# Attention as a stream of units with key features in place, and a second graph layer's bases added in halves beside the first layer

## What is computed

```python
xn = _layernorm(x, axis=-1)
x = x + gnn(xn) + mix(xn)          # graph layers; attention and perceptron, twice
x = x + ffn(_layernorm(x))         # memory layer: 64 rows of two tables per token

# gnn: two layers, relu between them
w = jnp.einsum('rb,bio->rio', att, basis)       # 2 relations from 30 bases of 512x512
gate = jax.nn.sigmoid(x_j @ gate_w[r, :, 0])    # for each relation
agg = jax.ops.segment_sum(msg, row)             # msg = gate * x_j @ w[r]
return agg + x @ root + bias

# mix, for each of 2 blocks, 8 heads of 64, 256 features
qp = ratio * (jnp.exp(q_dash - diag - rowmax) + 1e-4)
kp = ratio * (jnp.exp(k_dash - diag - globalmax) + 1e-4)
ctx = jnp.einsum('bhnm,bhnd->bhmd', kp, v)
o = jnp.einsum('bhmd,bhnm,bhn->bhnd', ctx, qp, 1 / (qp @ kp.sum(2)))
x = x + o @ Wo + bo; x = x + gelu(layernorm(x) @ W1 + b1) @ W2 + b2
```

## Time and profile before

| what | us |
|---|---|
| median of 3 runs (3040.13 to 3047.05) | 3040.56 |
| the profiled execution | 3042.31 |
| its span, first to last instruction | 3040.5 |
| TensorE busy | 2645.5 |
| VectorE busy | 1529.6 |
| GpSimd busy | 1021.6 |
| memory layer, from 1862 us to the end | 1178 |

### The profile page before, as it was taken

The page is one execution under the profiler, slowest core; times in us unless marked ns, Lnnn a source line. Parts: engine busy times, 40 slices in busy tenths (PEclk is TensorE's granted clock), DMA queues, the critical chain, the costliest instruction groups (busy, mean ns, idle before and its releaser), DMA issues.

```text
span 3040.5 us, 27921 instructions
## 1 busy us (share of the span) xinstructions
PE 2645.5 (87%) x8756; PEld 1455.5 (48%) x8756; DVE 1529.6 (50%) x3729; ACT 701.9 (23%) x1525; POOL 1021.6 (34%) x833
## 2 busy tenths in 40 slices
PE   3998887999199999999898887898998999998877
PEld 2664555666044444444565545554454444443322
DVE  4556457999400000000225543357666676676664
ACT  1223222211021001100235222133233333322222
POOL 0006686666000000000000000055656665665665
PEclk9998998999699999999999998999999999999999
DMA  8911416777902230243000400088988988998898
GB/s 284 276 41 4 111 1 169 207 206 216 213 29 56 66 83 0 64 116 93 7 0 0 155 0 7 7 280 314 327 308 308 337 317 302 339 328 320 320 346 331
DMA packets 243106, 523.84 MB, mean 172 GB/s; under 512 B 98857, under 2 KB 99232, under 8 KB 238850
## 3 DMA queue, kind: packets, MB, share of 16 engines
q0 software_dynamic: 161392, 348.53, 34.6%
q1 hardware_dynamic: 79072, 169.12, 17.8%
q10 hardware_dynamic: 2550, 5.12, 0.5%
HBM read 489.51 MB, written 45.34 MB: 176 GB/s over the span
## 4 chain that ended last, share of the span: by engine, by line
PE 66%; DVE 14%; issue 7%; DMA 6%; ACT 3%; POOL 1%; SPq 1%; another core or an unknown queue 1%; DVEq 0%; ACTq 0%; POOLq 0%
PE bank L1256 13%; PE bank L1029 10%; PE bank L1014 5%; DVE qv L863 4%; PE bank L1236 4%; PE bank L1246 4%; PE bank L781 3%; PE bank L561 2%; PE bank L1193 2%; PE bank L1019 2%; PE bank L573 2%; PE bank L568 2%; PE bank L592 2%; PE bank L808 2%; PE bank L1205 2%
## 5 line engine op out<-in xcount | busy, mean ns | idle before, releaser
L1156 POOL MEMSET wreg<- 64x2048 f32 x2 | 3.6, 1802 | 1106.9 <-DVE h L711 1106.9
L1256 PE MATMUL bank<-qv,stage 125*125 125x512 f32 x640 | 340.2, 623 | 37.9 <-issue 15.7
L1337 ACT ACTIVATE stage<-ident,qv 125x125 f32<-125x125 f32 x640 | 246.4, 399 | 507.9 <-DVE qv L1490 175.1
L1490 DVE SCALAR_TENSOR_TENSOR qv<-qv 125x512 f32<-125x512 f32 x320 | 237.9, 750 | 152.6 <-DMA qv<-in_L_ffn_rows,qv 69.1
L863 DVE SCALAR_TENSOR_TENSOR qv<-wreg,att_b,qv 128x2048 f32<-128x2048 f32 x120 | 276.8, 2348 | 48.8 <-DMA wreg<-in_L_gnn_basis 42.3
L287 POOL DMA_INDIRECT adj<-e_cnt,e_idx x80 | 176.3, 2204 | 310.0 <-issue 273.6
L1162 POOL DMA_INDIRECT qv<-in_L_ffn_rows,qv x160 | 162.3, 1015 | 221.3 <-DVE qv L1432 113.0
L287 POOL DMA_INDIRECT adj_b<-e_cnt,e_idx x80 | 180.7, 2258 | 71.0 <-DMA adj<-e_cnt,e_idx 39.8
L1256 PEld LDWEIGHTS bank<-qv,stage 125*125 125x125 f32 x640 | 113.6, 193 | 184.0 <-issue 121.1
L1162 POOL DMA_INDIRECT qv<-in_L_ffn_rows,biasb x160 | 163.4, 1021 | 100.8 <-PE bank L1256 74.1
L1256 PE MATMUL bank<-big,stage 125*125 125x512 f32 x320 | 167.0, 617 | 13.3 <-issue 6.4
(11 more groups left out here) (222 smaller groups left out, 4167.6 us busy)
## 6 DMA issues: line engine op xcount, KB each, us to landing
wreg<-in_L_gnn_basis SPq DMA_DIRECT2D x60, 1024.0 KB
big<-in_L_mix_W SPq DMA_DIRECT2D x4, 4096.0 KB
adj<-adj_b POOLq DMA_DIRECT2D x9, 1328.1 KB, 40.9
adj<-wreg SPq DMA_DIRECT2D x5, 2187.5 KB
adj_b<-wreg SPq DMA_DIRECT2D x5, 2187.5 KB
...
```

Source lines behind the costliest of these rows:

```text
L1256: nc.tensor.matmul(psum[7][0:P, :], diags[:, s % DRING, :], ring[s % RING][0:P, DIM:ROW], start=(s == 0), stop=(s == SLOTS - 1), skip_grou ...
L1337: nc.scalar.activation(diags[:, s % DRING, :], ident[0:P, 0:P], ACT.Relu, scale=inner[:, s:s + 1]).then_inc(p_diag, 1)
L1490: nc.vector.scalar_tensor_tensor(ring[s % RING][0:P, 0:DIM], ring[s % RING][0:P, 0:DIM], probs_of[t % 2].rearrange("p h k -> p (h k)")[:, ...
```

## The change

- `attn1`: no loop registers. The heads' squares are 8 matmuls of 250 columns with a selector as weights, ScalarE copies their result, and four transposes bring it back. The next pair's scaled transposes come after the third copy of key features and not after the fifth.
- `attn2`: the key features stay in `kdash`. The shift is the bias of eight exponentials of 256 columns a tile, in place; VectorE adds 1e-4 in two halves; TensorE reads values and features where they are. The contexts' copies are shared by VectorE and ScalarE and begin as each bank ends.
- `attn3`: 40 units in one stream, for all ten tiles. The transposes of three units of four go to bank 2, those of the fourth and the output product to bank 3. The end work of a tile stands between units of the next.
- `mlp`: only the 30 bases of layer 0 are added there, from a ring of three.
- `gcn`: the 30 bases of layer 1 are loaded as 60 halves by GpSimd, behind scatters and sums on its queue, into a ring of four, and added by VectorE in layer 0: three halves before the root add of each tile in the first half, four before each tile's aggregate add in the second. The transposes of tile t+1 stand between the relations of tile t. Layer 1 reads its input where it is. The weights and the first two tiles of x may come before the perceptron's end; layer 1's slabs may come before its first half ends; the second attention block no longer waits at its start for the stored result.

```diff
+        WREL_B = 5100
+        wrel = qv[:, :].rearrange("p (l k) -> p l k", l=2)[:, :, 0:4096].rearrange("p l (r k) -> p l r k", r=2)
...
+        HRING = 4
+        s_hload = [sem(f"half_basis_ring_{n}") for n in range(HRING)]
+        half_ring = [stage[:, 2024 + 1024 * n:3048 + 1024 * n] for n in range(HRING - 1)] + [ctx_flat[:, 0:1024]]
...
-        BLOCKS = 2 * BASES // PAIRS
-        BRING = 4
+        BLOCKS = BASES // PAIRS
+        BRING = 3
...
-                    if c == 0:
-                        pe.wait_ge(m["kd"], l * ADDS["kd"] + i * 8 + 4)
+                    if i and c < 2:
+                        pe.wait_ge(m["kd"], kd0 + 5 + c)
...
+                    else:
+                        pe.wait_ge(m["kd"], l * ADDS["kd"] + i * 8 + n + 1)
                     if n == 2:
-                        pe.wait_ge(m["k"], l * ADDS["k"] + i * KC + KC + 2)
-                    if n == 4 and not last:
+                        pe.wait_ge(m["dgc"], l * ADDS["dgc"] + i + 1)
+                        for jj in range(2):
+                            for s in range(2):
+                                mm = nc.tensor.transpose(psum[1][0:P, 256 * jj + 128 * s:256 * jj + 128 * s + 128],
+                                                         dgs[:, PT * s + P * jj:PT * s + P * jj + P], ident[:, :])
+                        mm.then_inc(m["dg_pe"], 1)
+                    if n == 4 and i < PAIRS - 1:
                         turn(i + 1)
-                    if n >= 4:
-                        pe.wait_ge(m["kd"], l * ADDS["kd"] + i * 8 + n + 1)
...
+                act.wait_ge(m["dg_mm"], l * ADDS["dg_mm"] + i + 1)
+                nc.scalar.activation(dgs, psum[0][:, 0:2 * PT], ACT.Copy).then_inc(m["dgc"], 1)
...
-                    if n == 5 and not last:
+                    if n == 3 and i < PAIRS - 1:
                         scale(i + 1)
...
         def attn2_act(act, l):
...
-            with act.Fori(0, PAIRS) as i:
-                for j in range(2):
-                    act.wait_ge(m["ctx_pe"], l * ADDS["ctx_pe"] + i * 2 + j + 1)
-                    nc.scalar.activation(v_st[:, j, :], v_aug[:, ds(i * 2 + j, 1), :, :].rearrange("p o h d -> p (o h d)"), ACT.Copy)
-                    act.wait_ge(m["ksub"], l * ADDS["ksub"] + i * 2 + j + 1)
-                    nc.scalar.activation(kfeat[:, j, :], sq1(kdash[:, ds(i * 2 + j, 1), :]), ACT.Exp).then_inc(m["kx"], 1)
+            for t in range(TILES):
+                for hh in range(HEADS):
+                    kt = kdash[:, t, FEATS * hh:FEATS * hh + FEATS]
+                    op = nc.scalar.activation(kt, kt, ACT.Exp, bias=kshift[:, t, hh:hh + 1])
+                    if hh % 4 == 3:
+                        op.then_inc(m["kx"], 1)
+            for b in (1, 3):
+                act.wait_ge(m["ctx_pe"], l * ADDS["ctx_pe"] + b + 1)
...
         def attn2_dve(dve, l):
-            def pair(i, last):
-                for j in range(2):
-                    dve.wait_ge(m["kx"], l * ADDS["kx"] + i * 2 + j + 1)
-                    nc.vector.tensor_scalar(kfeat[:, j, :], kfeat[:, j, :], EPS_K, None, ALU.add).then_inc(m["kf"], 1)
-                    if not last:
-                        subtract_k(dve, l, i * 2 + (2 + j))
-
-            with dve.Fori(0, PAIRS - 1) as i:
-                pair(i, False)
-            pair(PAIRS - 1, True)
-            dve.wait_ge(m["ctx_pe"], l * ADDS["ctx_pe"] + 2 + TILES)
-            for b in range(4):
+            for t in range(TILES):
+                for b in range(2):
...
-                    for hh in range(HEADS):
-                        mm = nc.tensor.matmul(psum[hh // 2][0:HD + 1, FEATS * (hh % 2):FEATS * (hh % 2) + FEATS],
-                                              v_st[:, j, (HD + 1) * hh:(HD + 1) * hh + HD + 1], kfeat[:, j, FEATS * hh:FEATS * hh + FEATS],
-                                              start=False, stop=True, skip_group_check=True)
...
-        QD_BANKS = (0, 1, 6, 7)
+            for t in range(TILES):
+                for hh in range(HEADS):
+                    if hh % 4 == 0:
+                        pe.wait_ge(m["kf"], l * ADDS["kf"] + 2 * t + hh // 4 + 1)
+                    mm = nc.tensor.matmul(psum[hh // 2][0:HD + 1, FEATS * (hh % 2):FEATS * (hh % 2) + FEATS],
+                                          v_aug[:, t, hh, :], kdash[:, t, FEATS * hh:FEATS * hh + FEATS],
...
+        def turn_bank(u):
+
+            return 3 if u % KC == 1 else 2
...
+                if 2 <= n < UNITS + 2:
+                    u = n - 2
+                    dve.wait_ge(m["qT_pe"], l * ADDS["qT_pe"] + u + 5)
+                    nc.vector.tensor_scalar(qfeat_t[:, u % 2, :], psum[turn_bank(u)][:, 0:4 * P], EPS_K, None, ALU.add).then_inc(m["qT"], 1)
+                if n >= 4 and n % 2 == 0 and (n - 4) // 4 < TILES:
+                    normalize((n - 4) // 4, (n - 4) % 4 // 2)
+                if n >= 10 and n % 4 == 2:
...
+                    residual((n - 10) // 4)

...
             if l == 0:
                 act.sem_inc(m["qT_pe"], 4)
...
+            def out_turn(T):
+                pe.wait_ge(m["o"], l * ADDS["o"] + 2 * T + 4)
...
+            for n in range(UNITS + 6):
+                if n < UNITS:
...
+                        pe.wait_ge(m["ctx"], l * ADDS["ctx"] + 4)
+                    pe.wait_ge(m["qx"], l * ADDS["qx"] + u + 5)
+                    if u % KC == 1 and u >= 9:
+                        pe.wait_ge(m["hat"], l * ADDS["hat"] + 2 * ((u - 9) // 4) + 3)
+                    elif u:
+                        pe.wait_ge(m["qT"], l * ADDS["qT"] + u + (1 if u % KC in (1, 2) else 2))
+                    for q in range(4):
+                        mm = nc.tensor.transpose(psum[turn_bank(u)][:, P * q:P * q + P], qfeat[:, u % 4, 128 * q:128 * q + 128], ident[0:P, 0:P])
+                    mm.then_inc(m["qT_pe"], 1)
...
+                if n >= 8 and n % 4 == 0:
+                    out_turn((n - 8) // 4)
+                if n >= 9 and n % 4 == 1:
+                    out_mm((n - 9) // 4)
...
-                    gl, b = n // (BLOCKS // 2), n % (BLOCKS // 2)
...
-                        nc.vector.scalar_tensor_tensor(wrel[:, gl, r, :], wreg[:, n % BRING, :], att_b[:, gl, ds(i * (BLOCKS // 2) + (r * BASES + b), 1)],
-                                                       wrel[:, gl, r, :], ALU.mult, ALU.add).then_inc(s_comb, 1)
+                        nc.vector.scalar_tensor_tensor(wrel[:, 0, r, :], wreg[:, n % BRING, :], att_b[:, 0, ds(i * BLOCKS + (r * BASES + n), 1)],
+                                                       wrel[:, 0, r, :], ALU.mult, ALU.add).then_inc(s_comb, 1)
...
             else:
-                sp.wait_ge(g_sem[0]["r"], 2 + TILES)
+                sp.wait_ge(g_sem[0]["r"], TILES)
             sp.dma_start(root_sb, a[f"L0_gnn_root{gl + 1}"].rearrange("(k p) n -> p k n", p=128)).then_inc(g["w"], 16)
...
-            sp.dma_start(b_g, a[f"L0_gnn_bias{gl + 1}"].partition_broadcast(P)).then_inc(g["w"], 16)
             if gl == 0:
-                with sp.Fori(0, PAIRS) as i:
-                    sp.wait_ge(g["xT_pe"], i * 2 + 2)
-                    sp.dma_start(gx, tok(xn_d)[:, ds(i * 2, 2), :]).then_inc(g["x"], 16)
-
-            def load_slab(i, j):
-                flat = slabs[gl][:, j, :, :].rearrange("p c r -> p (c r)")
+                sp.wait_ge(s_xnw, 32)
+                sp.wait_ge(m["y2_pe"], KC + KC * PAIRS)
+                for t in range(2):
+                    sp.dma_start(gx[:, t, :], tok(xn_d)[:, t, :]).then_inc(s_gx[t], 16)
+                sp.wait_ge(m["hf"], 2 + 2 * TILES)
+            sp.dma_start(b_g, a[f"L0_gnn_bias{gl + 1}"].partition_broadcast(P)).then_inc(g["b"], 16)
...
+            if gl == 1:
+                sp.wait_ge(g["r"], TILES)
+                sp.wait_ge(g_sem[0]["agg"], TILES)
+                attn_loads_sp(sp, 1)
...
+        def gcn_turn_pe(pe, gl, t):
+            g = g_sem[gl]
+            if gl == 0:
+                pe.wait_ge(s_gx[t % 2], 16 * (t // 2) + 16)
             else:
-                load_slab(0, 0)
-                sp.wait_ge(g["r"], 2 + TILES)
-                sp.wait_ge(g_sem[0]["agg"], 2 + TILES)
-                load_slab(0, 1)
...
+            for k in range(KC):
+                rows = gx[:, t % 2, 128 * k:128 * k + 128] if gl == 0 else x1[:, t, 128 * k:128 * k + 128]
+                mm = nc.tensor.transpose(psum[t % 2][:, P * k:P * k + P], rows, ident[0:P, 0:P])
+            mm.then_inc(g["xT_pe"], 1)
...
+                if gl == 0 and t == 1:
+                    pe.wait_ge(m["hf"], 2 + 2 * TILES)
+                for r in range(RELS):
+                    if t >= 2:
+                        pe.wait_ge(g["z"], 2 * (t - 2) + r + 1)
...
+                    if r == 0 and t < TILES - 1:
+                        gcn_turn_pe(pe, gl, t + 1)
+                if t >= 2:
+                    pe.wait_ge(g["r"], t - 1)
+                elif gl == 1:
+                    pe.wait_ge(g_sem[0]["out"], 2 * (TILES - 2 + t) + 1)
```

(46 more changed lines are left out.)

530 lines of the change are left out of this document (240 added, 290 removed).

## The result

The changed kernel takes **2807.88 us** (median of 4 runs, 2807.37 to 2809.99) against 3043.48 for the kernel before, a ratio of 0.9227 with a 95% interval of 0.9211 to 0.9243. The profiled execution's span is 2805.3 us; 3040.5 was that of before.

A forecast was written before the change was run, and what follows sets the result against it. TensorE, busy 87% of the span, was taken as the bound, so only its idle or slow time could be won: 53 + 35 + 21 + 50 + 31 = 190 us off 3040.5, forecast 2851 us, range 2818 to 2908.

The forecast's parts named there:

- Second step of attention: Attention's second step, both blocks: the shift as bias of the exponentials replaces VectorE's subtraction; 35 us won, bounds 20 and 38.
- First step: Attention's first step, both blocks: earlier scaled transposes end 20.2 us of waits, squares' products costed even; 21 us won.
- Third step: Attention's third step, both blocks: one stream of 40 units removes the stalls at pair ends; 53 us won, bounds 10 and 64.
- Rival 1: Attention's third step: stream bound by VectorE, a tile stalls 3.2 us instead of 1; 2895 us, chance 0.15.
- The gap: 72 us without TensorE work after the perceptron: 22 stay because of the adjacency sums, 50 us won, bounds 25 and 72.
- rival 2: First graph layer starved by base halves: sums end later than 760, or the ring runs dry; 2891 us, chance 0.16.
- The halves: Second layer's bases as 60 half loads: 120 adds of 1.28 us in the first graph layer, nothing on the path.
- The rest of the graph layers: Graph layers: hidden copies, shorter first halves and no wait before the second attention block; 31 us won, bounds 20 and 36.
- The memory layer: Everything from 1862 us on: same code before and after, its 1178 us would not move.
- rival 5: Better than forecast: the sums end before the perceptron and the attention stream has no stall; 2815 us, chance 0.1.

The follow-up runs named there:

- squares_one_group: The changed kernel with all eight products of the squares writing PSUM rows 0 to 31 instead of four row groups: 2831.84 us, 0.9346 of before.
- after_again: The changed kernel, unchanged, run again as the control of a later group on a different chip: 2785.21 us, 0.9255 of before.

## Why the prediction missed, step by step

**Second step of attention: right.** 35.8 us for 35, by the mechanism given.

**First step: mechanism incomplete, the term mis-sized (54 for 21).** The step that failed is that the squares' products, "16 products of 8 columns per pair that become 8 of 250 columns", were costed even. They were not even: the sixteen, each a load of 125 weight columns for 8 columns of data, cost TensorE 38.7 us over both blocks, and the eight cost 10.6. I had priced 250 columns as if TensorE were full while 32 weight columns stream; squares_one_group shows that this holds only when all write the same rows (35.7 us, near even), and that the four row groups are worth 24 us. The Trainium skill had the rule: page "TensorE: Matmul & The Clock Gate", section "Part 3: Packing small matmuls — row/col tiling": products whose outputs lie in different groups of 32 PSUM partitions run at the same time, each in its own part of the array. The runs here agree (1.05 against 3.57 us), and a look at the output's start partition in the diff would have been enough. The other terms: TensorE's idle time in this step was 18.2 us (from 186.00 less 175.07, and 172.00 less 164.76 in the kernel before) and is 2.5 now, 15.7 us won where the forecast counted 20.2. The added transposes cost 6 us, not 4. The products that are the same before and after took 14.0 us less over both blocks, at a granted clock of 1.00 and 0.99 instead of 0.92 and 0.96; the forecast had 5 for the clock. Together 28 + 16 + 14 less 6 are 52 of the 54 us. The clock's share was not tested apart.

Busy us and mean ns of one, first block before (and the second block's L580), then first block after; L592 and L600 are the same product:

```profile
L592 PE MATMUL bank<-projbd,stage 128*125 128x512 f32 x80 | 46.6, 731 | 1.3 <-ACT big L624 1.3
L580 PE MATMUL bank<-headsel,stage 128*125 128x8 f32 x160 | 20.0, 265 | 0.0
L580 PE MATMUL bank<-headsel,stage 128*125 128x8 f32 x160 | 18.7, 256 | 0.0
```

```profile
L600 PE MATMUL bank<-projbd,stage 128*125 128x512 f32 x80 | 37.4, 600 | 0.3 <-ACT big L632 0.3
L580 PE MATMUL bank<-stage,headsel 128*32 128x250 f32 x80 | 5.3, 380 | 0.0
```

The row of the first step before, same columns as the earlier trace rows:

```profile
55.00:241.00 186.00, 175.07 (x672) 119.44 (x672) 91.10 (x402) 54.04 (x115) 0.00 (x0) 0.92 0.56 169
1462.00:1634.00 172.00, 164.76 (x672) 114.47 (x672) 47.91 (x82) 54.10 (x115) 0.00 (x0) 0.96 0.00 0
```

**Third step: right mechanism, size 11 us off (63.6 for 53).** TensorE's timeline in the stream, where an output product (L774) comes every 13.30 us:

```profile
268.40 0.60 PE L766 MATMUL bank<-ident,stage 125*128 125x125 f32 x4
...
270.95 3.65 PE L774 MATMUL bank<-wreg,stage 128*125 128x512 f32 x8
...
278.26 0.62 PE L800 MATMUL bank<-ident,big 125*128 125x125 f32 x4 [0.64 <-DVE h L697]
...
284.25 3.65 PE L774 MATMUL bank<-wreg,stage 128*125 128x512 f32 x8
```

The stall that the single transposes bank costs is there, once a tile behind the residual add, but 0.64 us in place of 1, and filling and draining take 4 us and not 8 (137 less 133). Both together are 7 us a block. Rival 1, a stream bound by VectorE, is refuted: it needed 3.2 us a tile.

**The gap: 37.6 for 53.** Two steps failed. The first is "they need 52 us by themselves and about 70 with what shares the engines". The 241 GB/s behind the 52 were what sums and bases moved together; the sums had 7.63 MB of it in 45 us, 170 GB/s, and 188 in the changed kernel (5.08 MB in 27 us), which makes 66 us by themselves. From the issue at 661.1 to the first half base on VectorE at 745.8 they took 84.7 us, and 78.8 in after_again. The second is "TensorE starts the graph layer at 737 and not at 715: 22 of the 72 us stay": the perceptron was through at 682.5, 32 us earlier than forecast since the steps ahead had given more, but the sums began only 6 us earlier (661 for 667) and ended later, and 36.6 us of waits stayed. The price of an SP load was wrong too: the 15.1 us per MB of the earlier trace rows hold for bases of 128 rows, and a tile of 125 rows took 11.9 us for 250 KB, behind a bias load of the same size that the forecast did not count. What I had as the lower bound (25, "the first half loads, behind them on GpSimd's queue, keep VectorE from the root add that the third tile waits for") is what happened, so rival 2's first half was true, at a price of 15 us and not of 25; its second half, a ring that runs dry, was not: from the fourth tile on a tile takes 11.6 us.

**The halves: right.** 120 adds of 1.276 us (1.28 forecast), and none on the path outside the first tiles. GpSimd issued its loads without being held by VectorE's adds, 0.70 to 0.72 us each in the middle of them, as the forecast took from the earlier trace rows. The prediction had the Trainium skill speak against this placing; its page "SBUF — State Buffer", section "Who interferes with whom", gives copies, casts and `tensor_scalar` as operations that can enter the two-port modes, and does not name these adds. So the page and the trace do not differ here.

**The rest of the graph layers: right** (30.6 for 28; its own terms 133 and 5 less 117 are 21 and not 18, which makes 31). **The memory layer:** "the forecast is wrong if the memory layer's 1178 us move". They moved by 11.7 without the change. Without them the miss is 33 us, not 45: 33 in the first step (24 of them the row groups), 11 in the stream, 5 in the rest, less 15 for the gap. That the miss is not larger is luck, since the gap's error ran against the others. The result lies nearest to rival 5's 2815, but not by its way: the sums did not end before the perceptron.
